# Attention on row and column tiles of TensorE in a decoder layer on one Trainium2 core

## The chip, the core and the metric

The kernel runs on one core of one Trainium2 chip. The metric is the device time of one execution in microseconds, lower is better. Engines are named as in the profile: PE is TensorE (PEld its weight loads), DVE is VectorE, ACT is ScalarE, POOL is GpSimd, SP is SyncE, which here only issues DMAs.

## What is computed

A decoder layer on eight sequences of 100 tokens with 256 features, in float32: a bidirectional state space mixer, cross attention to a context of 361 tokens per sequence, and a mixture of eight experts. The change touches the cross attention alone. Cut to it, with 16 heads of 16 features:

```python
v = (values @ Wv.T).reshape(N, -1, HEADS, HEAD_DIM)
k = (keys @ Wk.T).reshape(N, -1, HEADS, HEAD_DIM)
q = (query @ Wq.T).reshape(N, -1, HEADS, HEAD_DIM)
energy = jnp.einsum('nqhd,nkhd->nhqk', q, k)
attn = jax.nn.softmax(energy / HEAD_DIM ** 0.5, axis=-1)
out = jnp.einsum('nhqk,nkhd->nqhd', attn, v).reshape(N, Q, EMBED)
return out @ Wo.T + bo
```

## The kernel before

The program is written out engine by engine, with semaphores between them; nothing is scheduled by a tool, each engine runs its instructions in the order of the code. Four stages follow each other: projections and convolution of the mixer, its scan over 256 steps (the longest), attention, and the experts.

Attention goes sequence by sequence (`b`), and in a sequence by eight groups `g` of two heads (`attend`). Features lie on partitions: head h holds 16 of them, so a tile of 128 partitions holds eight heads, and there are two such tiles (`m`). Keys and values of the next sequence are made between the groups of the present one. Numbers with the precision of float32 are split into a high and a low part of a faster type (`three`: high by high, high by low, low by high), for queries, keys, context and their weights.

- **Queries.** ScalarE copies the high part, VectorE makes the low part (`high_queries`, `low_queries`). GpSimd spreads them (`spread_queries`, L666): for each head a block of 100 columns in which the 112 rows of the other heads are zero. So a matmul over all 128 rows gives the scores of one head.
- **Scores** (`scores`, L1011 by `three`): for each of two heads three matmuls with 100 weight columns and 362 streamed columns, into one PSUM bank per head.
- **Softmax.** VectorE takes the maxima of two heads (`maxima`, L1626) and scales and negates them (L1629, `shift`); ScalarE takes the exponential with that bias and accumulates the sum (`mass`, L901), one instruction a head and a read of the accumulator behind it.
- **Turning** (`turn_probs`, L1170): six transposes per group; VectorE copies one head's result out (L1637), ScalarE the other's (L910).
- **Weighing** (`weigh_values`, L1186): the turned probabilities are the weights (100 columns), the values of a head are streamed (16 columns); an fp32 matmul is two passes, so twelve passes a group. Heads come out token-major.
- **Normalising.** VectorE takes the reciprocal of 16 sums per token (L1641) and multiplies (L1644), TensorE turns the heads back (`turn_heads`, L1195), VectorE copies (L1651), TensorE projects them (`project_heads`, L1202, two fp32 matmuls), VectorE adds (L1659).

The order on TensorE is: turn group g, scores of group g+2, keys or values of the next sequence (groups 2 to 5), weigh group g. Turning g+2 must wait for the exponentials of g+2 and for both copies of g+1. Sequences 1 to 6 run in a hardware loop on TensorE, ScalarE, VectorE and GpSimd. Before attention GpSimd splits weights and contexts and adds the output bias to the residual (L674).

The profile's names: `ps` is PSUM, `x_tok` the residual, `q_blk_h/_l` the spread queries, `kT_h/_l` the keys. Forms read out<-in; in a matmul's form 128*100 is rows by weight columns, and behind it rows by streamed columns.

## Time and profile before

| | us |
|---|---|
| median of 3 runs | 1297.92 (1297.28 to 1300.14) |
| the profiled execution | 1293.94 |
| its span, from the first to the last instruction | 1292.2 |
| TensorE busy in it | 1033.0 (80%) |
| VectorE busy | 925.3 (72%) |
| GpSimd busy | 782.5 (61%) |
| ScalarE busy | 542.0 (42%) |

The span's four stages have different limits, so shares over the span say little about one of them. Attention lies at about 830 to 1058 us; what it costs is read from that stretch. Times in the views are from the span's start. A row of the timeline merges instructions of one kind that follow each other.

### The profile page before, as it was taken

Reading aid. Unit: us, or ns where it says so; the run is one execution under the profiler, and the core shown is the slowest. Engines: PE = TensorE matmul, PEld = TensorE weight load, DVE = VectorE, ACT = ScalarE, POOL = GpSimd, SP = SyncE. Lnnn points to the kernel's source line nnn. Section 1 sums busy time; section 2 is a strip of 40 time slices with the busy share of each in tenths; the row PEclk is TensorE's granted clock in tenths of the full one; section 3 lists DMA queues with packets and bytes.
Section 4 is the critical chain, followed back from the end, with each engine's and each line's share of the span. In section 5 each row is a group of like instructions: output and inputs, shape, how many; then the busy total and the mean of one; then the engine's idle time right before and its main releaser. Section 6 shows DMA issues by size and latency. Waiting matters only on the chain.

```text
span 1292.2 us, 14793 instructions
## 1 busy us (share of the span) xinstructions
PE 1033.0 (80%) x4832; PEld 705.2 (55%) x4832; DVE 925.3 (72%) x1068; ACT 542.0 (42%) x1188; POOL 782.5 (61%) x469
## 2 busy tenths in 40 slices
PE   7596676767667676676765779889999979899996
PEld 5243333433334333343332447779999966499995
DVE  6978998998989989999999993666666652021111
ACT  2686443443444434444444431244444433133231
POOL 4255998998998989989899890555223000402112
...
DMA packets 95706, 131.70 MB, mean 102 GB/s; under 512 B 12153, under 2 KB 89098, under 8 KB 95626
## 3 DMA queue, kind: packets, MB, share of 16 engines
...
## 4 chain that ended last, share of the span: by engine, by line
PE 37%; DVE 27%; issue 26%; POOL 5%; ACT 1%; SPq 1%; another core or an unknown queue 1%; DMA 1%; DVEq 0%; POOLq 0%; ACTq 0%
DVE states L1538 13%; DVE states L1550 10%; PE ps L1011 6%; PE ps L1378 6%; PE ps L1392 5%; PE ps L1186 4%; PE ps L1004 3%; PE ps L1170 2%; PE ps L1078 2%; PE ps L1069 2%; PE ps L1315 2%; PE ps L1324 2%; POOL dt L596 1%; POOL dtu L600 1%; POOL row_sel L565 1%
## 5 line engine op out<-in xcount | busy, mean ns | idle before, releaser
L619 POOL TENSOR_TENSOR states<-states,c_row 128x800 f32<-128x800 f32 x255 | 474.4, 1883 | 58.7 <-DVE states L1550 57.7
L1550 DVE TENSOR_TENSOR_SCAN states<-ps,states 128x800 f32<-128x800 f32 x256 | 462.7, 1830 | 0.0
L852 ACT ACTIVATE ps<-dt,neg_a 128x396 f32<-128x396 f32 x512 | 283.4, 585 | 361.8 <-DVE states L1550 361.8
L1078 PE MATMUL ps<-states,ident 128*128 128x400 f32 x1024 | 417.1, 543 | 1.9 <-POOL states L619 1.9
L1078 PEld LDWEIGHTS ps<-states,ident 128*128 128x128 f32 x1024 | 211.2, 210 | 142.0 <-issue 52.4
L1538 DVE TENSOR_TENSOR states<-dtu,ps 128x800 f32<-128x800 f32 x192 | 188.1, 980 | 31.1 <-PE ps L1060 28.3
L1060 PE MATMUL ps<-b_parts,row_sel 96*128 96x400 bf16 x192 | 69.0, 360 | 161.8 <-DVE states L1538 156.3
L1060 PEld LDWEIGHTS ps<-b_parts,row_sel 96*128 96x128 bf16 x192 | 18.9, 99 | 237.6 <-DVE states L1538 220.1
L610 POOL TENSOR_TENSOR states<-dtu,b_row 128x800 f32<-128x800 f32 x64 | 121.1, 1892 | 0.0
L901 ACT ACTIVATE probs<-ps,shift 100x361 f32<-100x361 f32 x128 | 70.8, 559 | 99.1 <-DVE shift L1629 99.1
...
L971 ACT ACTIVATE hid_tile<-ps,w_tile 128x128 f32<-128x128 f32 x160 | 45.6, 368 | 97.8 <-PE ps L1378 97.8
L1186 PEld LDWEIGHTS ps<-v,probsT 128*100 128x100 f32 (+1 forms) x768 | 75.4, 168 | 10.9 <-issue 8.3
L666 POOL TENSOR_TENSOR q_blk_h<-qT_h,head_mask 128x800 fp32r<-128x800 f32 x16 | 24.4, 1524 | 91.2 <-PE ps L1011 81.4
L1186 PE MATMUL ps<-v,probsT 128*100 128x16 f32 (+1 forms) x768 | 74.9, 236 | 5.4 <-ACT probsT L910 4.6
L1378 PEld LDWEIGHTS ps<-x_turned,w_tile 128*128 128x128 f32 x640 | 75.4, 194 | 2.2 <-issue 1.3
L1378 PE MATMUL ps<-x_turned,w_tile 128*128 128x128 f32 x640 | 75.7, 277 | 1.0 <-DVE out_tok L1789 1.0
L1626 DVE TENSOR_REDUCE neg_max<-ps 100x2 f32<-100x722 f32 x64 | 58.1, 908 | 25.5 <-PE ps L1011 25.5
...
L1392 PE MATMUL ps<-w_tile,hid_tile 128*128 128x256 f32 x320 | 72.2, 379 | 0.0
L1392 PEld LDWEIGHTS ps<-w_tile,hid_tile 128*128 128x128 f32 x320 | 59.3, 190 | 7.3
L994 PE MATMUL ps<-xT,win 128*128 128x400 f32 x128 | 52.8, 579 | 7.4 <-ACT u_pad L753 7.4
...
## 6 DMA issues: line engine op xcount, KB each, us to landing
c_row<-rows SPq DMA_DIRECT2D x256, 200.0 KB, 3.1
...
```

What stands on the lines that cost most here:

```text
L610: nc.gpsimd.tensor_tensor(states[i % RING][:].rearrange("p (c t) -> p c t", c=CP), dtu[d][:, cp * CP:(cp + 1) * CP, chunk(q)], b_row[turn ...
L619: nc.gpsimd.tensor_tensor(st, st, c_row[i % C_SLOTS][:].unsqueeze(1).broadcast_to([P, CP, TQ]), ALU.mult).then_inc(product_ready, 1)
L852: nc.scalar.activation(seqs(decay[i % DECAYS][:, j * TQ:(j + 1) * TQ])[:, :, 1:], seqs(dt_sb[d][:, c, chunk(q)])[:, :, 1:], ACT.Exp, scale ...
L901: nc.scalar.activation(probs[g % 2][:, j, 0:S], ps[0:L, g % 2 * 2 + j, 0:S], ACT.Exp, bias=shift[:, r, h:h + 1], scale=HD ** -0.5, accum_o ...
L1011: mm = nc.tensor.matmul(to, w[i], x[j], start=(first and n == 0), stop=(last and n == 2))
L1060: nc.tensor.matmul(ps[:, 6 + turn % 2, 0:TQ], row_sel[:, n, :], b_parts[d][:, chunk(q)], start=True, stop=True).then_inc(b_bank_ready, 1)
L1078: mm = nc.tensor.matmul(ps[:, j, 0:TQ], ident[:], states[i % RING][:, j * TQ:(j + 1) * TQ], start=False, stop=(i % N == N - 1), skip_group ...
L1186: mm = nc.tensor.matmul(ps[0:L, 6, h * HD:(h + 1) * HD], probsT[g % 2][j][0:size, kt * L:(kt + 1) * L], v_sb[r][0:size, kt, h * HD:(h + 1) ...
L1378: mm = nc.tensor.matmul(ps[:, hid_bank(k, ft), ft % 4 * P:(ft % 4 + 1) * P], w[:, W1_AT + m * F + ft * P:W1_AT + m * F + (ft + 1) * P], x_ ...
L1392: mm = nc.tensor.matmul(ps[:, 6 + k % 2, 0:D], hid_tile[k % 2][:, ft, :], w[:, W2_AT + ft * D:W2_AT + (ft + 1) * D], start=(ft == 0), stop ...
L1538: nc.vector.tensor_tensor(states[i % RING][:].rearrange("p (c t) -> p c t", c=CP), dtu[d][:, cp * CP:(cp + 1) * CP, chunk(q)], ps[:, bank_ ...
L1550: nc.vector.tensor_tensor_scan(st, decay[i % DECAYS], st, 0.0, ALU.mult, ALU.add).then_inc(scan_done, 1)
```

## The change

Queries are kept twice, once masked to the even heads of each 32 rows and once to the odd ones (`q_part`, masks `par_mask`, which also carry the factor 1/4 of the scores), so that a matmul over 32 rows gives the scores of one head. The two heads of a group lie in different 32-row tiles. GpSimd no longer spreads queries. Values are kept in 32 columns a head: 16 values, a one, and zeros; they become the weights, and the turned probabilities are streamed (100 columns), into a 32-partition strip of PSUM for each head. The column of ones makes the sums. The heads come out feature-major, so they are not turned; one matmul with a selecting matrix spreads the sums over each head's partitions, and the reciprocal and the product run on 128x400. The output weights are spread over four blocks to match, which makes the projection four fp32 matmuls. Maxima come negated, without the scaling. TensorE's loop over sequences is written out.

```diff
-KEY_BANK = 7
+KEY_BANK, HEAD_BANK = 7, 6
+QUAD = 32
+PAR = QUAD // HD
+BLOCKS = H // (P // QUAD)
+HEAD_CONSTS = 7
...
-        qT_part = [sb(f"qT_{n}", [P, KD, T], F32R, scope=attn) for n in "hl"]
-        q_blk = [[sb(f"q_blk_{n}{r}", [P, KD, HT, L], F32R, scope=attn) for n in "hl"] for r in range(2)]
+        q_part = [[sb(f"q_{n}{i}", [P, KD, T], F32R, scope=attn) for n in "hl"] for i in range(PAR)]
...
-        v_sb = [sb(f"v{r}", [P, KT, D], scope=attn) for r in range(2)]
+        v_sb = [sb(f"v{r}", [P, KT, H, QUAD], scope=attn) for r in range(2)]
...
-        neg_max, shift, mass, inv_mass = (
-            sb(n, [L, 2, H], scope=attn) for n in ("neg_max", "shift", "mass", "inv_mass"))
-        heads_tok = sb("heads_tok", [L, D], scope=attn)
-        headsT = sb("headsT", [P, KD, L], scope=attn)
+        neg_max = sb("neg_max", [L, 2, H], scope=attn)
+        heads_raw, inv_mass, headsT = (sb(n, [P, BLOCKS, L], scope=attn) for n in ("heads_raw", "inv_mass", "headsT"))
+        mass_sel = sb("mass_sel", [P, P], scope=attn)
...
+        def head_at(pos):
+
+            m, rest = divmod(pos, HT)
+            par, j = divmod(rest, P // QUAD)
+            return m, j, par
...
-            for w_dram, w_sbuf in ((wqT, wq_sb), (wkT, wk_sb), (wvT, wv_sb), (woT, wo_sb)):
+            for w_dram, w_sbuf in ((wqT, wq_sb), (wkT, wk_sb), (wvT, wv_sb)):
...
+            sp.wait_ge(wo_zeroed, 1)
+            for m in range(KD):
+                for j in range(P // QUAD):
+                    sp.dma_start(wo_sb[j * QUAD:j * QUAD + HD, m * PAR:(m + 1) * PAR, :],
+                                 woT.rearrange("(m j r i) e -> m j i r e", m=KD, j=P // QUAD, r=PAR)[m, j]
+                                 ).then_inc(wo_in, 16)
...
-            fill(head_mask[:], 1.0)
+            fill(head_mask[:], HD ** -0.5)
...
-            pool.wait_ge(attnw_in, 16 * 4)
+            job_result(pool, ("mix", DIRS - 1, B // 2 - 1))
+            nc.gpsimd.memset(wo_sb[:], 0.0).then_inc(wo_zeroed, 1)
+            nc.gpsimd.memset(mass_sel[:], 0.0).then_inc(sel_ready, 1)
+            for r in range(2):
+                nc.gpsimd.memset(v_sb[r][:], 0.0).then_inc(v_zeroed, 1)
+            pool.wait_ge(sel_ready, 1)
+            selected = mass_sel[:].rearrange("p (j i) -> p j i", i=QUAD)
+            nc.gpsimd.affine_select(out=selected, in_=selected, compare_op=ALU.not_equal, fill=1.0, base=-HD,
+                                    pattern=[[-QUAD, P // QUAD], [0, QUAD]], channel_multiplier=1
+                                    ).then_inc(sel_ready, 1)
+            pool.wait_ge(v_zeroed, 2)
+            for r in range(2):
+                nc.gpsimd.memset(v_sb[r][:, :, :, HD:HD + 1], 1.0).then_inc(v_zeroed, 1)
+            pool.wait_ge(attnw_in, 16 * 3)
...
-            def spread_queries(b, r):
-
-                for m in range(KD):
-                    if isinstance(b, int):
-                        job_copied(pool, ("qT", m, b // BQ))
-                    for part, block in zip(qT_part, q_blk[r]):
-                        nc.gpsimd.tensor_tensor(
-                            block[:, m],
-                            part[:, m, bass.ds(b * L, L)].bitcast(F32).unsqueeze(1).broadcast_to([P, HT, L]),
-                            head_mask[:].unsqueeze(2).broadcast_to([P, HT, L]), ALU.mult).then_inc(q_blk_ready, 1)
-
-            spread_queries(0, 0)
...
-            spread_queries(1, 1)
...
-            def prepare(b, r, next_loads=None):
-
-                pool.wait_ge(scores_ready, GROUPS * b - GROUPS)
-                spread_queries(b, r)
-                if next_loads is not None:
-                    split_context(b + 1, 1 - r, next_loads)
+            def prepare(b, r, next_loads):
+
+                split_context(b + 1, 1 - r, next_loads)
...
-                nc.scalar.activation(qT_part[0][:, m, chunk(q)], bank(("qT", m, q))[:, 0:TQ], ACT.Copy
-                                     ).then_inc(q_high, 1)
-
+                for i in range(PAR):
+                    ins = nc.scalar.activation(q_part[i][0][:, m, chunk(q)], bank(("qT", m, q))[:, 0:TQ],
+                                               ACT.Identity, scale=par_mask[:, i:i + 1])
+                ins.then_inc(q_high, 1)
...
-                act.wait_ge(shift_ready, GROUPS * b + (g + 1))
+                act.wait_ge(max_ready, GROUPS * b + (g + 1))
...
-                                         bias=shift[:, r, h:h + 1], scale=HD ** -0.5,
-                                         accum_out=mass[:, r, h:h + 1]).then_inc(probs_ready, 1)
+                                         bias=neg_max[:, r, h:h + 1]).then_inc(probs_ready, 1)
...
             def scores(b, r, g):
                 m = 2 * g // HT
-                pe.wait_ge(q_blk_ready, 2 * KD * b + 2 * (m + 1))
                 if g % (GROUPS // KD) == 0:
                     pe.wait_ge(k_copied, 2 * b + (m + 1))
                 if not isinstance(b, int) or GROUPS * b + g >= 2:
 
                     pe.wait_ge(probs_ready, 2 * GROUPS * b + (2 * g - 2))
-                for j in range(2):
-                    mm = three(ps[0:L, g % 2 * 2 + j, 0:SE], [part[:, m, (2 * g + j) % HT, :] for part in q_blk[r]],
-                               [part[:, m, :] for part in kT_part[r]], True, True)
+                for n, (hi, lo) in enumerate(((0, 0), (0, 1), (1, 0))):
+                    for i in range(2):
+                        _, j, par = head_at(2 * g + i)
+                        rows = slice(j * QUAD, (j + 1) * QUAD)
+                        mm = nc.tensor.matmul(ps[0:L, g % 2 * 2 + i, 0:SE],
+                                              q_part[par][hi][rows, m, b * L:(b + 1) * L],
+                                              kT_part[r][lo][rows, m, :], start=(n == 0), stop=(n == 2))
                 mm.then_inc(scores_ready, 1)
...
-                for j in range(2):
-                    h = 2 * g + j
-                    for kt in range(KT):
-                        size = P if kt < KT - 1 else SL
-                        mm = nc.tensor.matmul(ps[0:L, 6, h * HD:(h + 1) * HD],
-                                              probsT[g % 2][j][0:size, kt * L:(kt + 1) * L],
-                                              v_sb[r][0:size, kt, h * HD:(h + 1) * HD],
+                for kt in range(KT):
+                    size = P if kt < KT - 1 else SL
+                    for i in range(2):
+                        m, j, par = head_at(2 * g + i)
+                        block = (2 * g + i) // (P // QUAD)
+                        mm = nc.tensor.matmul(ps[j * QUAD:(j + 1) * QUAD, HEAD_BANK, block * L:(block + 1) * L],
+                                              v_sb[r][0:size, kt, m * HT + j * PAR + par, :],
+                                              probsT[g % 2][i][0:size, kt * L:(kt + 1) * L],
                                               start=(kt == 0), stop=(kt == KT - 1))
                 mm.then_inc(pv_done, 1)
...
-            def turn_heads(b):
+            def spread_mass(b):
                 pe.wait_ge(heads_ready, b + 1)
-                for m in range(KD):
-                    mm = nc.tensor.transpose(ps[:, KEY_BANK, m * L:(m + 1) * L], heads_tok[:, tile(m)],
-                                             ident[0:L, 0:L])
-                mm.then_inc(headsT_done, 1)
+                nc.tensor.matmul(ps[:, KEY_BANK, 0:BLOCKS * L], mass_sel[:], heads_raw[:].rearrange("p k t -> p (k t)"),
+                                 start=True, stop=True).then_inc(mass_spread, 1)
 
             def project_heads(b):
                 pe.wait_ge(headsT_copied, b + 1)
-                for m in range(KD):
-                    mm = nc.tensor.matmul(ps[0:L, KEY_BANK, 0:D], headsT[:, m, :], wo_sb[:, m, :], start=(m == 0),
-                                          stop=(m == KD - 1))
+                if b == 0:
+                    pe.wait_ge(wo_in, 16 * KD * (P // QUAD))
+                for k in range(BLOCKS):
+                    mm = nc.tensor.matmul(ps[0:L, KEY_BANK, 0:D], headsT[:, k, :], wo_sb[:, k, :], start=(k == 0),
+                                          stop=(k == BLOCKS - 1))
                 mm.then_inc(wo_done, 1)
...
-            with pe.Fori(0, B // 2 - 1) as i:
-                attend(2 * i + 1, 1)
-                attend(2 * i + 2, 0)
+            for b in range(1, B - 1):
+                attend(b, b % 2)
...
-            dve.wait_ge(consts, TURNS)
+            dve.wait_ge(consts, HEAD_CONSTS)
+            nc.vector.tensor_reduce(par_mask[:], head_mask[:].rearrange("p (j r) -> p r j", r=PAR), AX.X, ALU.add
+                                    ).then_inc(mask_ready, 1)
...
-                nc.vector.tensor_tensor(qT_part[1][:, m, chunk(q)], bank(("qT", m, q))[:, 0:TQ],
-                                        qT_part[0][:, m, chunk(q)].bitcast(F32), ALU.subtract
-                                        ).then_inc(copied["v"], 1)
-
+                for i in range(PAR):
+                    ins = nc.vector.scalar_tensor_tensor(
+                        q_part[i][1][:, m, chunk(q)], bank(("qT", m, q))[:, 0:TQ], par_mask[:, i:i + 1],
+                        q_part[i][0][:, m, chunk(q)].bitcast(F32), ALU.mult, ALU.subtract)
+                ins.then_inc(copied["v"], 1)
...
             def maxima(b, r, g):
                 dve.wait_ge(scores_ready, GROUPS * b + (g + 1))
                 nc.vector.tensor_reduce(neg_max[:, r, 2 * g:2 * g + 2], ps[0:L, g % 2 * 2:g % 2 * 2 + 2, 0:S],
-                                        AX.X, ALU.max).then_inc(max_ready, 1)
-                dve.wait_ge(max_ready, GROUPS * b + (g + 1))
-                nc.vector.tensor_scalar(shift[:, r, 2 * g:2 * g + 2], neg_max[:, r, 2 * g:2 * g + 2],
-                                        -HD ** -0.5, None, ALU.mult).then_inc(shift_ready, 1)
+                                        AX.X, ALU.max, negate=True).then_inc(max_ready, 1)
...
-            def normalise_heads(b, r):
-                dve.wait_ge(probs_ready, 2 * GROUPS * b + 2 * GROUPS)
-                nc.vector.reciprocal(inv_mass[:, r, :], mass[:, r, :]).then_inc(inv_mass_ready, 1)
+            def copy_heads(b):
+                dve.wait_ge(pv_done, GROUPS * b + GROUPS)
+                nc.vector.tensor_copy(heads_raw[:].rearrange("p k t -> p (k t)"), ps[:, HEAD_BANK, 0:BLOCKS * L]
+                                      ).then_inc(heads_ready, 1)
+
+            def normalise_heads(b):
+                dve.wait_ge(mass_spread, b + 1)
+                nc.vector.reciprocal(inv_mass[:].rearrange("p k t -> p (k t)"), ps[:, KEY_BANK, 0:BLOCKS * L]
+                                     ).then_inc(inv_mass_ready, 1)
                 dve.wait_ge(inv_mass_ready, b + 1)
-                dve.wait_ge(pv_done, GROUPS * b + GROUPS)
-                nc.vector.tensor_tensor(heads_tok[:].rearrange("l (h e) -> l h e", h=H),
-                                        ps[0:L, 6, 0:D].rearrange("l (h e) -> l h e", h=H),
-                                        inv_mass[:, r, :].unsqueeze(2).broadcast_to([L, H, HD]), ALU.mult
-                                        ).then_inc(heads_ready, 1)
-
-            def copy_heads(b):
-                dve.wait_ge(headsT_done, b + 1)
-                nc.vector.tensor_copy(headsT[:].rearrange("p m t -> p (m t)"), ps[:, KEY_BANK, 0:KD * L]
-                                      ).then_inc(headsT_copied, 1)
+                nc.vector.tensor_tensor(headsT[:], heads_raw[:], inv_mass[:], ALU.mult).then_inc(headsT_copied, 1)
```

In the order of instructions the change shows at three places. TensorE, one group with neither keys nor values, in the middle of a sequence (turning, scores, weighing), before:

```order
L1170 MATMUL ps<-ident,probs 128x100 x6
L1011 MATMUL ps<-kT_h,q_blk_h 100x362
L1011 MATMUL ps<-kT_l,q_blk_h 100x362
L1011 MATMUL ps<-kT_h,q_blk_l 100x362
L1011 MATMUL ps<-kT_h,q_blk_h 100x362
L1011 MATMUL ps<-kT_l,q_blk_h 100x362
L1011 MATMUL ps<-kT_h,q_blk_l 100x362
```

and after, with the weighing and the next group's turning:

```order
L1191 MATMUL ps<-ident,probs 128x100 x6
L1179 MATMUL ps<-kT_h,q_h 100x362 x2
L1179 MATMUL ps<-kT_l,q_h 100x362 x2
L1179 MATMUL ps<-kT_h,q_l 100x362 x2
L1208 MATMUL ps<-probsT,v 32x100 x6
L1191 MATMUL ps<-ident,probs 128x100 x6
```

The six score matmuls now alternate between the two heads, each pair in two row tiles, and weighing writes 32 rows by 100 columns where it wrote 100 by 16.

VectorE, from the last maxima of a sequence's groups to the addition of the attention's output, before:

```order
L1626 TENSOR_REDUCE neg_max<-ps 100x2
L1629 TENSOR_SCALAR shift<-neg_max 100x2
L1641 RECIPROCAL inv_mass<-mass 100x16
L1644 TENSOR_TENSOR heads_tok<-ps,inv_mass 100x256
L1637 COPY probsT<-ps 128x300
L1626 TENSOR_REDUCE neg_max<-ps 100x2
L1629 TENSOR_SCALAR shift<-neg_max 100x2
L1651 COPY headsT<-ps 128x200
L1637 COPY probsT<-ps 128x300
L1626 TENSOR_REDUCE neg_max<-ps 100x2
L1629 TENSOR_SCALAR shift<-neg_max 100x2
L1659 TENSOR_TENSOR x_tok<-x_tok,ps 100x256
```

and after:

```order
L1654 TENSOR_REDUCE neg_max<-ps 100x2
L1666 COPY heads_raw<-ps 128x400
L1662 COPY probsT<-ps 128x300
L1654 TENSOR_REDUCE neg_max<-ps 100x2
L1671 RECIPROCAL inv_mass<-ps 128x400
L1674 TENSOR_TENSOR headsT<-heads_raw,inv_mass 128x400
L1662 COPY probsT<-ps 128x300
L1654 TENSOR_REDUCE neg_max<-ps 100x2
L1681 TENSOR_TENSOR x_tok<-x_tok,ps 100x256
```

The reciprocal moved behind the maxima of group 2 of the next sequence, on 128x400, with the product right behind it and ahead of the next copy.

GpSimd, from its last product of the scan to the split of the key weights, after (before, the row of L657 followed the first one directly, as L637):

```order
L652 TENSOR_TENSOR states<-states,c_row 128x400
L670 MEMSET wo_sb 128x1024
L671 MEMSET mass_sel 128x128
L673 MEMSET v 128x1536 x2
L676 AFFINE_SELECT mass_sel<-mass_sel 128x128
L681 MEMSET v 128x48 x2
L657 TENSOR_TENSOR wk_h<-wk_sb,one 128x512
```

Seven instructions stand between the scan and the splits.

## Rows read from the trace of the kernel before

**Rows 1.** Busy time of each engine in a stretch of attention, clock, DMA

```profile
core 0: us, PE busy (x) PEld busy (x) DVE busy (x) ACT busy (x) POOL busy (x), PEclk, DMA share, GB/s
900.00:950.00 50.00, 49.36 (x436) 47.53 (x435) 31.16 (x62) 24.59 (x79) 14.88 (x11) 1.00 0.06 16
```

**Rows 2.** Timeline of TensorE: start us, us, engine, line, out<-in, count

```profile
902.75 0.71 PE L1170 MATMUL ps<-ident,probs 100*128 100x100 f32 x6
...
904.28 1.02 PE L1202 MATMUL ps<-wo_sb,headsT 128*100 128x256 f32 x4
905.15 1.15 PE L1186 MATMUL ps<-v,probsT 128*100 128x16 f32 x12
...
913.33 0.71 PE L1170 MATMUL ps<-ident,probs 100*128 100x100 f32 x6
913.82 0.39 PE L1011 MATMUL ps<-kT_h,q_blk_h 128*100 128x362 f32 x1
...
914.86 0.29 PE L1011 MATMUL ps<-wv_h,ctx_h 128*128 128x256 f32 x1
...
916.29 1.15 PE L1186 MATMUL ps<-v,probsT 128*100 128x16 f32 x12
...
929.23 0.71 PE L1170 MATMUL ps<-ident,probs 100*128 100x100 f32 x6
```

**Rows 3.** Timeline of all engines, groups 6 and 7; waits in brackets

```profile
920.54 0.71 PE L1170 MATMUL ps<-ident,probs 100*128 100x100 f32 x6
...
922.27 0.91 DVE L1626 TENSOR_REDUCE neg_max<-ps 100x2 f32<-100x722 f32 x1 [0.52 <-PE ps L1011]
...
923.22 0.48 DVE L1629 TENSOR_SCALAR shift<-neg_max 100x2 f32<-100x2 f32 x1
...
923.81 0.56 ACT L901 ACTIVATE probs<-ps,shift 100x361 f32<-100x361 f32 x1 [1.53 <-DVE shift L1629]
...
924.27 0.19 ACT L901 ACTIVATION_READ_ACCUMULATOR probs<-ps,shift 100x1 f32 x1
...
924.89 0.42 ACT L910 ACTIVATE probsT<-ps 128x300 f32<-128x300 f32 x1
...
925.46 1.20 PE L1186 MATMUL ps<-v,probsT 128*100 128x16 f32 x12 [0.29 <-ACT probsT L910]
...
926.51 0.71 PE L1170 MATMUL ps<-ident,probs 100*128 100x100 f32 x6
```

**Rows 4.** Groups of VectorE by shape: busy us, mean ns, idle before, releaser

```profile
L1641 DVE RECIPROCAL inv_mass<-mass 100x16 f32<-100x16 f32 x8 | 1.9, 243 | 0.0
...
L1445 DVE RECIPROCAL rstd<-std 100x4 f32<-100x4 f32 x10 | 1.8, 178 | 7.7 <-ACT std L749 7.7
L1795 DVE COPY shared_sum<-ps 128x400 f32<-128x400 f32 x2 | 1.1, 575 | 31.1 <-PE ps L1345 31.1
```

**Rows 5.** Timeline of TensorE in the expert stage

```profile
1108.15 1.51 PE L1315 MATMUL ps<-xn3T,w_shared 128*128 128x400 f32 x4
1109.59 1.54 PE L1302 MATMUL ps<-ident,rows_src 100*9 100x100 f32 x16
1111.06 1.61 PE L1324 MATMUL ps<-hidden,w_shared 128*128 128x400 f32 x4
...
1128.61 2.95 PE L1345 MATMUL ps<-cwT,b_sb 9*128 9x400 f32 x8
1131.50 0.66 PE L1366 MATMUL ps<-ident,x_tile 128*128 128x128 f32 x4
```

**Rows 6.** As rows 1, while TensorE runs matmuls on 16 rows (form 16*128)

```profile
66.00:70.00 4.00, 4.00 (x7) 1.99 (x7) 3.00 (x7) 2.85 (x6) 0.00 (x0) 0.50 0.22 51
```

**Rows 7.** Timeline beside GpSimd's fill early on, and before attention's first turning

```profile
19.65 8.42 DVE L1470 TENSOR_SCALAR diag_d<-ident,vec 128x128 f32<-128x128 f32 x8
...
20.44 3.52 POOL L558 MEMSET row_sel<- 96x4096 bf16 x1 [16.16 <-DMA bias_tok<-in_bo]
...
839.95 3.66 DVE L1629 TENSOR_SCALAR shift<-neg_max 100x2 f32<-100x2 f32 x1
...
846.58 0.62 PE L1170 MATMUL ps<-ident,probs 100*128 100x100 f32 x5 [3.18 <-DVE qT_l L1604]
```

34 lines of the change are left out of this document (22 added, 12 removed).

## Prediction

> **What bounds the kernel now.** I read the stretches first, then TensorE's timeline in one sequence, then the waits behind its idle time. From 846 us to 1055 us the kernel does attention, one of the eight sequences after the other, and there TensorE is busy 49.4 of 50 us at full clock, VectorE 31.2, ScalarE 24.6, GpSimd 14.9 [rows 1]. So this stage belongs to TensorE, and its cost is read from where the same instruction comes back: transposing the probabilities of head pair 1 starts at 902.75 and, one sequence later, at 929.23, so a sequence takes 26.48 us [rows 2]. Inside a group (one pair of heads) the parts are: six transposes 0.49 us (913.33 to 913.82), six score matmuls 1.04 (to 914.86: 0.165 each and 0.06 for weights that weren't loaded ahead), the values of the next sequence 1.43 for twelve (so 0.71 for six), weighing the values, and elsewhere the output projection, 0.87 for four passes (904.28 to 905.15) [rows 2]. Keys are six matmuls of the scores' form, so 0.99.
>
> Not every group is full. Groups 6, 7 and 0 have little between scores and weighing, and there a loop of latencies decides: transposes of group g (920.54), scores of g+2, their maxima (922.27, 0.91 us), the shift (923.22), two exponentials (923.81), ScalarE's copy of the probabilities of g+1 (924.89, 0.42), weighing g+1 (925.46), transposes of g+2 (926.51): 5.97 us for two groups [rows 3]. In it the shift lasted 0.48 us where a free one takes 0.17, since GpSimd was spreading queries; without that the pair is 5.66.
>
> **Scores.** The block-masked queries on 128 rows become masked queries on 32 rows: the same six matmuls of 362 columns, three for each of two heads, but the two heads lie in different row tiles. If two tiles run at once, three slots of 0.165 replace six: 0.50 for 0.99. If not, nothing is gained. No row of before has two matmuls at different tile positions, so this is bounded from both sides, by 0.50 and 0.99; I take 0.50. The Trainium skill, "TensorE: Matmul & The Clock Gate", Part 3 (Measured speedup vs the span model), gives 3.07 times for four row tiles and 2.38 times for three column tiles; no run here shows it yet.
>
> **Weighing.** Twelve passes (an fp32 matmul is two) now load 100 weight columns to stream 16 columns: 1.05 us (925.46 to 926.51) [rows 3]. Afterwards each loads 32 and streams 100. The rows have exactly such passes, 9 weight columns and 100 streamed, at 0.086 us (1.54 us is 15 steps and one pass of 0.25) [rows 5]. Serial, twelve are 1.03, no gain. In two column tiles the second pass of one head runs beside the first of the other: seven slots, 0.60. I take 0.60, bound 1.03.
>
> **Switching.** This is the price that the change adds. Every group now goes from the whole array to row tiles to column tiles and back, with keys and values as one more change. Before has a handful of such changes [rows 5]: four matmuls from 1108.15 would end at 1109.49 at their pace of 0.336, the narrow ones start at 1109.59 (0.10); sixteen of them need 1.38 and the next line starts 1.47 later (0.09), and its first four last 1.61 instead of 1.51 (0.10 for weights that can't be loaded ahead). Eight matmuls on 9 rows need 2.69 and take 2.89: 0.20 in and out. So a change is 0.10, and behind it the first weights: 0.03 for 32 columns or the transposes, 0.10 for the whole array, and before the scores two loads of 100 columns, between 0.08 (the two at once) and 0.17 (twelve loads in 1.05, so 0.087 each, one after the other); I take 0.15 in the sum below and come back to it.
>
> **One sequence afterwards.** A plain group on TensorE: 0.49 + (0.10 + 0.15 + 0.50) + (0.10 + 0.03 + 0.60) + 0.13 = 2.10. Two groups with keys: 2 x (2.10 + 0.99 + 0.20) = 6.58. Two with values: 2.10 + 1.43 + 0.20 = 3.73 and 2.10 + 0.71 + 0.20 = 3.01. Groups 6 and 7 go by the loop: 0.49 + 0.10 + 0.15 + 0.50 + 0.17 for the last score to finish + 0.03, maxima 0.91 + 0.03, exponentials, copy 0.42, 0.15 until weighing, 0.60 + 0.13. The exponentials take 1.08 as a pair now (923.81 to 924.89) and lose two reads of the accumulator of 0.20 each [rows 3], most of which overlaps the exponential: 0.98, bounds 0.69 and 1.08. Sum 4.65. That is 1.3 less than 5.97, and TensorE waits 0.2 per group.
>
> Groups 0 and 1 of the next sequence carry the heads' end. Spreading the masses is one matmul of 400 columns, two passes, 0.67 + 0.20: group 0 is 2.97. Then VectorE, behind the maxima, takes a reciprocal of 128x400 where it took one of 100x16. A reciprocal of 4 columns is 178 ns and one of 16 is 243 [rows 4]: 5.4 ns for each further column, so 178 + 396 x 5.4 = 2.3 us. Its lower bound is the copy of 128x400, 0.57 [rows 4]; I take the slope. The multiply is another 0.57. From the transposes of group 0 on: maxima end 1.44 + 0.91 = 2.35, reciprocal 4.7, multiply 5.3, and only then the projection, now eight passes instead of four, 1.74 + 0.10 (TensorE alone would be there at 4.1), then 0.86 for weighing and the way back: 8.0 for groups 0 and 1. Total 6.58 + 3.73 + 3.01 + 4.65 + 8.0 = 25.97, against 26.48: **0.5 us less per sequence**, with half of TensorE's score and weighing work gone. With the reciprocal at 0.57 it would be 24.97.
> The Trainium skill, "VectorE: DVE Perf Modes" (First, the fixed hardware budget), says that the divide runs with a repeat count of 8; at the 0.96 GHz that it gives, 400 columns would be an estimated 3.3 us. Rows 4 say 5.4 ns, and the sum goes by them.
>
> **Around the sequences.** Seven periods: -3.7. The last sequence has groups 2 to 7 without keys or values, two and a half pairs at 5.66 - 4.65: -2.5. Groups 0 and 1 of the first one: one pair, -1.3. Before them TensorE stood 3.2 us at 846.58, because a shift lay 3.66 us behind GpSimd's bias addition [rows 7]; now there is no shift, and GpSimd, freed of 32 multiplies of 1.5 us, adds the bias some 6 us sooner. The queries now cost two ScalarE and two VectorE instructions for one, 1.1 us of it on this path: -2.0. The end: after the last weighing VectorE had 0.42 and 0.37 us of work and two transposes; now a copy of 0.57, the mass at half clock 1.5, reciprocal 2.3, multiply 0.57, less 0.5 for a shorter last weighing: +3.5. The longer projection hides behind the first half's normalisation.
> Two costs come from GpSimd blocking VectorE's SBUF-to-SBUF instructions. Eight scalings that need 1.6 us lasted 8.42 us beside a fill of 3.52 [rows 7]. At 806 us GpSimd now clears four tiles, some 4,200 columns at 0.86 ns (3.52 us for 4,096), 3.7 us while VectorE normalises what TensorE waits for; it would wait for about one of the two large fills, 1.3: +1.1, bounds 0 and 3.7. And the new sum of the mask stands ahead of those eight scalings, so one instruction fewer slips through before the fill: +0.5, bounds -1 and +1. The eight small loads of the output weights come on SP's queue behind the context and ahead of the shared weights, which wait for 828 us anyway, and nothing needs them for 30 us: 0. TensorE's loop written out takes away three branches at the ends of passes and register steps that TensorE's queue ran ahead of: 0.
> Sum: -3.7 - 2.5 - 1.3 - 2.0 + 3.5 + 1.1 + 0.5 = -4.4. If weights of two row tiles load together, the six full groups of each sequence save 0.07, about -3 in all; I take half, -1.5. That makes **-6**: the profiled execution (1293.9 with its ends) would be 1288, and against the median of 1297.9 the forecast is **1292**. By itself this case reaches from 1283 (quick reciprocal) to 1301 (the bounds of the clearing and of the weights).
>
> **The rivals.**
> The tiles don't overlap. Then only the switches are bought. Each group costs 0.49 + 0.43 more than above; groups 6 and 7 are then TensorE's (6.04 instead of 4.65) and 0 and 1 rise by 0.9: 26.0 + 3.7 + 1.4 + 0.9 = 32.0, or 5.5 more than before, seven times 38, and the ends add 4: 1340. The whole span between 0.5 us of gain and 5.5 of loss per sequence hangs on the share of slots that overlap, so this mechanism decides already where less than nine tenths of them do: at half, the kernel is some 18 us slower. Nothing in the profile speaks for or against it. That is the case on the other side.
> One of the two overlaps: 28.9 per sequence, 18 us more: 1316. Two-pass fp32 matmuls are the likelier ones to fail, since passes of one tile must follow each other.
> The clock falls. Sixteen matmuls on 16 rows ran at 0.50, with TensorE busy 4.00 of 4.00 us [rows 6], while this stage shows 1.00 [rows 1]. Afterwards half of the score and weighing time uses half of the array. At half clock the 19 us of matmul work per sequence double, 155 us for all; in a fifth of the stage it is 30 us: 1322 or more. Against it: transposes, keys and values stay whole, and the stage held 1.00 through weighing passes that streamed 16 columns.
> No change worth measuring: the forecast's mechanism, but the reciprocal and the clearing at their upper ends, 1297.
>
> **How the numbers follow.** Both overlap at full clock 0.66, with 1292; one 0.13, with 1316; none 0.12, with 1340; clock 0.09. A measurement of this kernel tells about 0.2% (2.6 us) from no change. Of the 0.66, 0.44 lie below 1295.3, 0.14 within 2.6 us of before, 0.08 above. So faster 0.44, same 0.14, slower 0.42. The range goes from 1283 to 1340; outside are most of the clock's case and the tails of the first.
>
> **What would show it.** Score matmuls of a pair starting within some 20 ns of each other at 0.165 per pair, weighing in about 0.6 us per group, and 0.1 us gaps at each change of shape confirm the first steps; equal spacing of 0.165 refutes. The reciprocal's row should read about 2,300 ns, and TensorE's longest idle time should stand before the projection and be put down to VectorE. Granted clock below 1.00 between 846 and 1050 us would make the forecast wrong, and so would changes of shape that cost twice as much: they stand 30 times in a sequence (three in a group, one more where keys, values, masses or the projection stand between), and 0.05 us each is 1.5 us, more than the whole gain.

## The result, and the profile after

| | us |
|---|---|
| median of 12 runs before | 1298.78 (1293.19 to 1300.78) |
| median of 12 runs after | 1289.78 (1287.41 to 1297.08) |
| ratio | 0.9946, 95% interval 0.9926 to 0.9966 |
| profiled execution after, and its span | 1289.13, 1287.4 |

The change makes the kernel 0.5% faster (0.7% by the medians). The twelve runs after spread over 10 us, and TensorE's clock goes with it: the four runs at 1295 to 1297 us have a mean granted clock of 0.906 to 0.909, the other eight, at 1287 to 1290.5, of 0.910 to 0.914. The kernel before spreads too, over 7.6 us. The profiled execution of before, 1293.94 us, is 4.8 below its median, that of after 0.7 below; so the two profiles differ by 4.8 us where the medians differ by 9.0, and what follows explains the 4.8.

**Two tiles work at once.** TensorE in groups 6 and 7 of a sequence, after. Columns as in [rows 2]; the bracket is what the engine waited for.

```profile
864.23 0.73 PE L1191 MATMUL ps<-ident,probs 100*128 100x100 f32 x6
864.89 0.41 PE L1179 MATMUL ps<-kT_h,q_h 32*100 32x362 f32 x2
865.14 0.33 PE L1179 MATMUL ps<-kT_l,q_h 32*100 32x362 f32 x2
865.30 0.33 PE L1179 MATMUL ps<-kT_h,q_l 32*100 32x362 f32 x2
865.56 0.71 PE L1208 MATMUL ps<-probsT,v 128*32 128x100 f32 x12
866.20 0.73 PE L1191 MATMUL ps<-ident,probs 100*128 100x100 f32 x6
```

A row with x2 is two score matmuls, one in each tile, that start together, and the next pair starts 0.16 us later (865.14, 865.30): two matmuls in a slot of 0.165, where in [rows 2] each took a slot of its own. From start to start, turning takes 0.66 us, the scores 0.67 and weighing 0.64, each with the change behind it: 1.97 us for a group that took 2.5. The first two weights of the scores load together too (PEld is the weight load):

```profile
864.89 0.16 PEld L1179 LDWEIGHTS ps<-kT_h,q_h 32*100 32x100 f32 x2
```

**The wait before the projection.** Groups 0 and 1, all engines, after:

```profile
896.62 2.66 DVE L1671 RECIPROCAL inv_mass<-ps 128x400 f32<-128x400 f32 x1
...
899.31 0.58 DVE L1674 TENSOR_TENSOR headsT<-heads_raw,inv_mass 128x400 f32<-128x400 f32 x1
...
899.94 2.98 PE L1224 MATMUL ps<-wo_sb,headsT 128*100 128x256 f32 x8 [1.38 <-DVE headsT L1674]
```

The waits of TensorE in attention (what waited, for what: us in total, times, longest) show that this one repeats, once behind each of the first seven sequences:

```profile
PE ps L1224 <- DVE headsT L1674: 9.7, 7, 1.4
PE ps L1208 <- ACT probsT L927: 5.2, 10, 0.6
```

**The clock behind it.** Busy time by stretch, columns as in [rows 1], clock third from the end:

```profile
896.00:900.00 4.00, 2.62 (x27) 1.51 (x25) 3.96 (x4) 1.44 (x3) 0.00 (x0) 1.00 0.00 0
900.00:904.00 4.00, 4.00 (x20) 2.46 (x20) 1.51 (x3) 1.01 (x2) 0.00 (x0) 0.59 0.00 0
904.00:908.00 4.00, 4.00 (x40) 3.11 (x40) 1.52 (x3) 1.80 (x4) 0.00 (x0) 0.98 0.00 0
```

Projection and the next weighing then run at half clock. Behind three of the seven waits it is so, behind four it isn't. One of each kind, by the starts of groups 1 and 2 (6.84 us and 5.32):

```profile
897.16 0.73 PE L1191 MATMUL ps<-ident,probs 100*128 100x100 f32 x6
904.00 0.53 PE L1191 MATMUL ps<-ident,probs 100*128 100x100 f32 x3
...
951.35 0.73 PE L1191 MATMUL ps<-ident,probs 100*128 100x100 f32 x6
956.67 0.73 PE L1191 MATMUL ps<-ident,probs 100*128 100x100 f32 x6
```

From start to start of each group's turning, in a sequence at full clock (us):

| group | 0 | 1 | 2 | 3 | 4 | 5 | 6 | 7 | sum |
|---|---|---|---|---|---|---|---|---|---|
| before | 2.72 | 3.40 | 3.52 | 3.64 | 3.97 | 3.25 | 2.93 | 3.04 | 26.5 |
| after | 2.84 | 5.33 | 3.16 | 3.17 | 3.59 | 2.86 | 1.98 | 2.60 | 25.5 |

**GpSimd's clearings.** After, VectorE and GpSimd (start, us):

```profile
806.68 2.70 POOL L673 MEMSET v<- 128x1536 f32 x2
...
808.17 1.23 DVE L1463 TENSOR_SCALAR var_eps<-moments 100x4 f32<-100x4 f32 x1
```

and the stretch behind it, before and after:

```profile
812.00:818.00 6.00, 6.00 (x26) 4.83 (x26) 1.21 (x3) 0.44 (x1) 5.55 (x9) 0.78 0.14 50
```

```profile
812.00:818.00 6.00, 6.00 (x22) 4.87 (x21) 1.77 (x3) 0.69 (x1) 5.76 (x10) 0.50 0.24 51
```

An instruction of 0.17 us (`var_eps`) lasted 1.23, until the second clearing was over; the gap on TensorE grew by as much (2.58 us for 1.52), and behind it the clock was at 0.50 where it had been at 0.78. From the end of this gap to the first queries' product TensorE needs 20.6 us, before 18.9.

**The tail.** Last weighing, and what follows, after:

```profile
1047.06 0.71 PE L1208 MATMUL ps<-probsT,v 128*32 128x100 f32 x12 [0.60 <-DVE probsT L1662]
1047.81 0.57 DVE L1666 COPY heads_raw<-ps 128x400 f32<-128x400 f32 x1 [0.84 <-PE ps L1208]
...
1048.44 0.94 PE L1216 MATMUL ps<-heads_raw,mass_sel 128*128 128x400 f32 x2 [0.67 <-DVE heads_raw L1666]
1049.41 2.66 DVE L1671 RECIPROCAL inv_mass<-ps 128x400 f32<-128x400 f32 x1 [1.03 <-PE ps L1216]
...
1052.74 3.74 PE L1224 MATMUL ps<-wo_sb,headsT 128*100 128x256 f32 x8 [3.36 <-DVE headsT L1674]
...
1056.58 0.42 DVE L1681 TENSOR_TENSOR x_tok<-x_tok,ps 100x256 f32<-100x256 f32 x1
```

### The profile page after: what moved, and what is told of

It reads as the page before. It is cut to its first block, busy times and chain, and to the rows that moved or that the text cites. A ratio compares the mean times of both kernels' runs of the same rounds, so it can differ in the third digit from the quotient of the medians.

```text
span 1287.4 us, 14434 instructions
## 1 busy us (share of the span) xinstructions
PE 1012.4 (79%) x4864; PEld 645.4 (50%) x4864; DVE 929.8 (72%) x1009; ACT 536.0 (42%) x1064; POOL 739.4 (57%) x444
## 4 chain that ended last, share of the span: by engine, by line
DVE 29%; issue 27%; PE 24%; DMA 10%; POOL 6%; ACT 1%; SPq 1%; DVEq 0%; POOLq 0%; ACTq 0%
DVE states L1561 13%; DVE states L1573 10%; DMA sums<-y_tile,x_tile 9%; PE ps L1021 3%; PE ps L1028 3%; PE ps L1208 3%; PE ps L1191 3%; PE ps L1095 2%; PE ps L1179 2%; PE ps L1086 2%; DVE inv_mass L1671 2%; POOL dt L616 1%; PE ps L1224 1%; POOL dtu L620 1%; POOL rows_by_slot L746 1%
## 5 line engine op out<-in xcount | busy, mean ns | idle before, releaser
L1561 DVE TENSOR_TENSOR states<-dtu,ps 128x800 f32<-128x800 f32 x192 | 185.4, 966 | 31.1 <-PE ps L1077 28.3
L919 ACT ACTIVATE probs<-ps,neg_max 100x361 f32<-100x361 f32 x128 | 64.9, 560 | 79.4 <-DVE neg_max L1654 79.4
L657 POOL TENSOR_TENSOR ctx_h<-ctx,one 128x722 fp32r<-128x722 f32 x8 | 11.1, 1390 | 107.4 <-PE ps L1028 94.9
L1825 DVE COPY x_turned<-ps 128x256 f32<-128x256 f32 x20 | 8.5, 425 | 67.7 <-PE ps L1387 67.7
L1837 DVE TENSOR_SCALAR y_tile<-ps,weight 128x256 f32<-128x256 f32 x20 | 9.7, 484 | 59.8 <-PE ps L1413 59.8
```

The lines of the kernel that those rows point to most:

```text
L919: nc.scalar.activation(probs[g % 2][:, j, 0:S], ps[0:L, g % 2 * 2 + j, 0:S], ACT.Exp, bias=neg_max[:, r, h:h + 1]).then_inc(probs_ready, 1)
L1561: nc.vector.tensor_tensor(states[i % RING][:].rearrange("p (c t) -> p c t", c=CP), dtu[d][:, cp * CP:(cp + 1) * CP, chunk(q)], ps[:, bank_ ...
```

## The experiments

Each median stands beside runs of the kernel before on the same chip, whose medians were 1297.3 to 1298.6 us. Ratios are to those.

### Is it overlap? One tile for both heads, and head by head

```diff
-            par, j = divmod(rest, P // QUAD)
+            j, par = divmod(rest, PAR)
...
-                        block = (2 * g + i) // (P // QUAD)
+                        block = m * PAR + par
```

> The two heads of a group lie in the same 32 rows and the same 32 columns (the pairing of heads is changed; weighing goes head by head), so nothing can overlap, while every matmul keeps its size and every change of shape stays. Theory (what the new forms gain is that two tiles work at once): three more score slots of 0.165 us and five more weighing slots of 0.086 us in a group, +0.92 us in each of groups 2 to 5, 1.2 in groups 6 and 7 together, 0.9 in groups 0 and 1, so +5.8 us per sequence and a median near 1335 us at full clock. Rival (a matmul on 32 rows or in 32 columns is quicker by itself): 1290 us. Second rival (with a quarter of the array at work at a time the clock falls, as in the run with the scores alone): half clock through attention, over 1400 us.

1340.85 us (1335.03 to 1342.17), ratio 1.0324 (1.0301 to 1.0347). Its TensorE, a plain group:

```profile
944.61 0.73 PE L1191 MATMUL ps<-ident,probs 100*128 100x100 f32 x6
945.27 0.57 PE L1179 MATMUL ps<-kT_h,q_h 32*100 32x362 f32 x2
945.68 0.48 PE L1179 MATMUL ps<-kT_l,q_h 32*100 32x362 f32 x2
946.01 0.48 PE L1179 MATMUL ps<-kT_h,q_l 32*100 32x362 f32 x2
946.43 1.22 PE L1208 MATMUL ps<-probsT,v 128*32 128x100 f32 x12
```

A pair of scores now takes 0.33 us from start to next start where it took 0.165, and weighing 1.15 to the next turning instead of 0.64. Sizes are the same, so the whole gain of the new forms is overlap: a sequence takes 31.9 us instead of 25.5, and the medians differ by 51. This is the rival "no overlap" of the prediction: its 32.0 us per sequence is right. That its total of 1340 is met to the microsecond is luck, since this execution has some 8 us at half clock in the first sequence (granted clock 0.74 from 847 to 880 us), which that sum had not.

```diff
-                for n, (hi, lo) in enumerate(((0, 0), (0, 1), (1, 0))):
-                    for i in range(2):
+                for i in range(2):
+                    for n, (hi, lo) in enumerate(((0, 0), (0, 1), (1, 0))):
```

and `i` ahead of `kt` in `weigh_values` in the same way.

> The kernel after, with the matmuls of a group in another order: all three score matmuls of the first head, then those of the second, and weighing likewise. Tiles, sizes and changes of shape are those of after. Theory (only neighbours in the queue overlap): scores take five slots of 0.165 us instead of three (+0.33), weighing eleven of 0.086 instead of seven (+0.34); +0.67 in each of groups 2 to 5, +0.7 in groups 6 and 7 together, +0.7 in groups 0 and 1, so +4 us per sequence and a median near 1321 us. Rival (each tile has its own queue and the second head catches up): 1290 us. Second rival (the gain is not overlap): 1290 us as well, told apart by the starts of the matmuls.

1299.74 us (1293.82 to 1302.84), ratio 1.0004 (0.9986 to 1.0021). The theory fails for the scores and in size for weighing, and the rivals' 1290 fails too. Scores lose nothing, weighing loses 0.20:

```profile
932.47 0.41 PE L1179 MATMUL ps<-kT_h,q_h 32*100 32x362 f32 x2
932.72 0.33 PE L1179 MATMUL ps<-kT_l,q_h 32*100 32x362 f32 x2
932.89 0.32 PE L1179 MATMUL ps<-kT_h,q_l 32*100 32x362 f32 x2
...
934.33 0.91 PE L1208 MATMUL ps<-probsT,v 128*32 128x100 f32 x12
```

The timeline lists matmuls by their start, and the second head's first still starts with the first head's first, though two more of the first head stand between them in the program. So a pair needn't be neighbours: the other tile's work is reached past three matmuls at once, and past the six passes of a head's weighing 0.20 us late. One sequence takes 26.7 us instead of 25.5, 1.2 more, where I had expected 4.

### Which half pays? Scores alone, values alone

```diff
-                for kt in range(KT):
-                    size = P if kt < KT - 1 else SL
-                    for i in range(2):
-                        m, j, par = head_at(2 * g + i)
...
-                        mm = nc.tensor.matmul(ps[j * QUAD:(j + 1) * QUAD, HEAD_BANK, block * L:(block + 1) * L],
+                for i in range(2):
+                    m, j, par = head_at(2 * g + i)
+                    h = m * HT + j * PAR + par
...
+                        mm = nc.tensor.matmul(ps[0:L, HEAD_BANK, h * HD:(h + 1) * HD],
+                                              probsT[g % 2][i][0:size, kt * L:(kt + 1) * L],
+                                              v_sb[r][0:size, kt, h * HD:(h + 1) * HD],
```

and the heads' end, the sums and the loads of before with it.

> Masked queries on 32 rows, negated maxima and the unrolled loop as in the kernel after; weighing, sums, heads and projection as in the kernel before (100 weight columns, 16 streamed; reciprocal on 100x16; no clearings on GpSimd). Theory (the scores pay, and the half for the values gives its gain back in the reciprocal, the longer projection, the clearings and the clock): groups 2 to 5 about 0.25 us shorter than before each, groups 6 and 7 0.75 together, groups 0 and 1 0.4, so 2 us less per sequence than before and a median near 1281 us, below the kernel after. Rival (both halves pay, the switches eat the one as the other): between before and after, 1294 us; TensorE busy without a gap and at full clock in either case.

1422.71 us (1421.08 to 1424.52), ratio 1.0972 (1.0940 to 1.1004): 125 us slower than before, and neither theory had it. The stretch 910 to 940 us of this kernel, and of the next one:

```profile
910.00:940.00 30.00, 30.00 (x157) 25.21 (x158) 10.33 (x18) 8.81 (x27) 2.97 (x2) 0.50 0.05 13
```

```profile
910.00:940.00 30.00, 29.67 (x274) 25.71 (x273) 17.36 (x29) 15.80 (x49) 2.98 (x2) 1.00 0.05 13
```

TensorE is busy 30 of 30 us and at half clock, and stays so from the second sequence to the last, 44.4 us each. The next kernel streams 64 columns of the values in a pass instead of 16, and nothing else differs; its heads come out wrong:

```diff
-                        mm = nc.tensor.matmul(ps[0:L, HEAD_BANK, h * HD:(h + 1) * HD],
+                        mm = nc.tensor.matmul(ps[0:L, HEAD_BANK, at:at + 64],
...
-                                              v_sb[r][0:size, kt, h * HD:(h + 1) * HD],
+                                              v_sb[r][0:size, kt, at:at + 64],
```

> The kernel with the scores alone in small tiles (label scores_only), and each weighing pass streams 64 columns of the values instead of 16, so that results of other heads are overwritten: the heads are wrong, the instructions, their order and their waits are the same. At full clock a pass is bound by its 100 weight columns (0.087 us) either way. Theory (it was the weighing's 16 streamed columns, next to scores on 32 rows, that left TensorE too little at work to keep its clock, not the small tiles): full clock in most of attention and a median between 1275 and 1290 us. Rival (the small tiles bring the clock down, whatever streams beside them, unless the weights too are in small tiles): half clock throughout, the passes bound by their weights, and 1423 us as before.

1286.37 us (1279.54 to 1294.54), ratio 0.9916 (0.9888 to 0.9944), as the theory had it. More work per instruction, 136 us less time. The weighing of both, by shape (busy us, mean ns):

```profile
L1186 PE MATMUL ps<-v,probsT 128*100 128x16 f32 x128 | 25.4, 319 | 0.0
```

```profile
L1187 PE MATMUL ps<-v,probsT 128*100 128x64 f32 x264 | 33.6, 250 | 1.3 <-ACT probsT L906 1.3
```

So small tiles do not lower the clock by themselves (one_tile kept 1.00 with a quarter of the array at work), and passes that stream 16 columns do not either while the scores fill the array [rows 1]. Both together do. In the first sequence this kernel too runs at half clock, from 846 to 865 us; why isn't tested. At full clock the scores alone take 24.7 us a sequence.

The other half, in `scores` and with `spread_queries` back on GpSimd:

```diff
-                                              q_part[par][hi][rows, m, b * L:(b + 1) * L],
-                                              kT_part[r][lo][rows, m, :], start=(n == 0), stop=(n == 2))
+                    mm = three(ps[0:L, g % 2 * 2 + i, 0:SE], [part[:, m, j * PAR + par, :] for part in q_blk[r]],
+                               [part[:, m, :] for part in kT_part[r]], True, True)
```

> The other half alone: values as weights in 32 columns, sums by the column of ones, spreading, reciprocal and projection as in the kernel after; scores on 128 rows with queries spread by GpSimd as in the kernel before. Theory A (the clock fell in the run with the scores alone because its weighing streamed 16 columns between scores on 32 rows; here scores fill the array): full clock but for stretches behind the projection's wait; groups 2 to 5 0.35 us shorter than before each, groups 6 and 7 0.7 together, groups 0 and 1 2.4 longer: +0.3 us per sequence, a median near 1301 us. Theory B (any small tile brings the clock down if it stands beside other work of little activity): half clock through attention, 1400 us or more.

1294.42 us (1292.46 to 1298.89), ratio 0.9974 (0.9962 to 0.9986), full clock through attention; 26.65 us a sequence, groups 0 and 1 8.45 of it. Theory A holds on the clock, and was 7 us too high on the time: the first sequence is 3.8 us shorter than before's, and the expert stage gives 2 us, which the sum had not. The halves don't add up: alone they give +125 and -4 us, together -9. Wide weighing is what keeps the clock for the small scores.

### Does the wait for the reciprocal bring the clock down?

```diff
-                nc.vector.reciprocal(inv_mass[:].rearrange("p k t -> p (k t)"), ps[:, KEY_BANK, 0:BLOCKS * L]
+                nc.vector.tensor_copy(inv_mass[:].rearrange("p k t -> p (k t)"), ps[:, KEY_BANK, 0:BLOCKS * L]
```

> The kernel after with a plain copy of 128x400 where the reciprocal stood, so the heads are not divided by their sums; nothing else differs. Theory (the reciprocal of 2.66 us makes TensorE wait 1.38 us before each projection, and that wait brings the clock down behind it in some sequences): the wait disappears, 7 x 1.38 = 9.7 us, the tail is 2.1 us shorter, no stretch at half clock behind a projection, 4.5 us more: a median near 1273 us and no run above 1277. Rival (the clock has nothing to do with the wait): the half-clock stretches stay, 1278 us. Second rival (another wait stands right behind, the copies of pair 1): 1285 us or more.

1276.82 us (1276.36 to 1278.04), ratio 0.9850 (0.9823 to 0.9877), and its four runs lie within 1.7 us. This kernel leaves the division by the sums out. TensorE's waits for `headsT` shrink to one, at the tail:

```profile
PE ps L1224 <- DVE headsT L1674: 1.3, 1, 1.3
```

The stretches at half clock behind the projections are gone and the runs no longer spread. It is 3.8 above the theory; the profiled execution has another stretch at half clock, in the first sequence, which is 3.9 us longer than in after.

```diff
+                    for _ in range(7):
+                        nc.tensor.matmul(ps[:, HEAD_BANK, 400:500], mass_sel[:], heads_raw[:, 0, :], start=True,
+                                         stop=True)
                     project_heads(b)
```

> The kernel after with seven more matmuls of 128 weight columns and 100 streamed columns (float32, 0.17 us each) between the scores of group 3 and the projection of the previous heads, in each sequence but the last; their result goes to unused columns of PSUM. TensorE is then busy in 1.2 of the 1.39 us that it waited; no step is taken out. Theory (the idle 1.4 us bring the clock down, at some places, in some executions): granted clock 1.00 behind every projection but for the first sequence, the spread between runs shrinks from 10 us to about 3, median near 1285 to 1287 us. Rival (the clock falls for the small tiles, or for something outside): half-clock stretches stay, median 1290 us with runs at 1296 us as before.

1289.28 us (1281.07 to 1290.27), ratio 0.9924 (0.9902 to 0.9946). No stretch at half clock behind a projection in the profiled execution, and no run above 1290.3; but the spread is 9 us where theory had 3, and the median didn't fall. Each sequence costs 0.1 us more, and the first sequence's stretch (3.9 us) is in this execution and was not in the profiled one of after. That filling the wait protects the clock is not shown by this: a kernel further down, `clear_late`, keeps the same seven waits unfilled,

```profile
PE ps L1223 <- DVE headsT L1673: 9.7, 7, 1.4
```

and has no stretch at half clock behind any of them either; headwise has one behind its seven waits of 1.2 us. So a wait of this length is followed by half clock only sometimes. What taking it away does is shown: the five kernels without it (copy_for_recip, warm, reordered, reordered_late, warm_late, of four or five runs each) have no stretch behind a projection, and runs within 1.4 to 3.5 us.

```diff
             queries(1)
+            pe.wait_ge(probs_ready, 4)
+            for _ in range(13):
+                nc.tensor.matmul(ps[:, 0, 400:500], mass_sel[:], ident[:, 0:L], start=True, stop=True)
```

> The kernel with the projection one group later (label reordered), and thirteen more matmuls of 128 weight columns and 100 streamed columns behind the last queries, where TensorE waits 2.6 us before the first turning; their result goes to unused columns of PSUM. Theory (that idle time brings the half-clock stretch of groups 1 and 2 of the first sequence: they took 3.49 and 5.47 us where later ones take 1.98 and 5.25): groups 0 to 2 of the first sequence about 1.5 to 3 us shorter, median near 1277 us. Rival (the stretch comes from the turn of the work to small tiles itself): no change, 1279 us.

This is the kernel `reordered`, shown below, with thirteen more matmuls. 1275.88 us (1275.26 to 1278.12) against 1279.24 (1278.39 to 1279.81) without them: 3.4 us less by medians from two chips; by the ratios to before on each, 0.9839 (0.9825 to 0.9854) and 0.9849 (0.9834 to 0.9863), it is little more than 1 us and within their intervals. The profiled executions differ by 4.2. The same 4 us of the first sequence, without and with:

```profile
848.00:852.00 4.00, 4.00 (x34) 2.80 (x29) 1.96 (x3) 1.70 (x4) 0.00 (x0) 0.51 1.09 326
```

```profile
848.00:852.00 4.00, 3.52 (x44) 2.46 (x38) 2.35 (x4) 2.65 (x6) 0.00 (x0) 1.00 1.10 330
```

Groups 0 to 2 of the first sequence take 7.5 us instead of 11.0. Such a stretch is in six of the nine profiled executions that leave this wait unfilled (scores_only and wide_stream aside), and in neither of the two that fill it. So thirteen matmuls with no use most likely shorten the kernel, as theory had it; by how much isn't settled.

### Do the clearings cost what they seem to?

```diff
-            nc.gpsimd.memset(wo_sb[:], 0.0).then_inc(wo_zeroed, 1)
...
             for n, (part, raw) in enumerate(((wk_part, wk_sb), (wv_part, wv_sb))):
                 split_into([t[:] for t in part], raw[:], kv_split, 2 * n)
...
-            for b in range(2):
-                split_context(b, b, 1)
+            nc.gpsimd.memset(wo_sb[:], 0.0).then_inc(wo_zeroed, 1)
...
+            split_context(0, 0, 1)
```

> The kernel after with the seven clearing and selecting instructions of GpSimd behind the splits of the key and value weights instead of ahead of them, and the split of the second context behind the addition of the output bias. Theory (a clearing holds VectorE's SBUF instruction for 1.06 us at 808.2 us, and the longer gap on TensorE brings its clock down for 1.6 us more): the first turning of attention 2.6 us earlier, median near 1287 us. Rival 1 (only the 1.06 us come back, the clock falls anyway): 1288.7. Rival 2 (the clearings now stand in the way of the contexts or of the next normalisation): 1290 or more.

1292.14 us (1283.68 to 1295.08), ratio 0.9947 (0.9929 to 0.9965). The median is that of the second rival and 5 us above the theory, but with a spread of 11 us it says little. In the profiled execution `var_eps` is back at 0.17 us:

```profile
807.60 0.17 DVE L1462 TENSOR_SCALAR var_eps<-moments 100x4 f32<-100x4 f32 x1
```

and the first queries' product starts at 828.6 us instead of 831.9; 0.6 of this it had already ahead of the clearings, so the edit gives 2.7, as the theory had it: 1.06 of the wait and 1.6 of the clock behind it. Against it stands the first sequence's stretch at half clock, 3.9 us, which this execution has and that of after has not.

All profiled executions together say how firm the second part is. From the end of TensorE's gap to the first queries' product it needs 20.0 to 20.6 us in seven of the eight executions whose gap is 2.58 us or more, and 18.9 in one (`filled_bank6`); where the gap is 1.52 us, it needs 18.9 in five of six, before among them, and 20.5 in one (`reordered_late`). So the longer gap mostly brings the lower clock with it, not always.

### A better order

The projection moves behind the scores of group 4, and the reciprocal is cut in two with `copy_probs` of group 1 between the halves:

```diff
                     scores(*nxt, 3)
-                    project_heads(b)
                     weigh_values(*nxt, 1)
+                    turn_probs(b + 1, 2)
+                    scores(*nxt, 4)
+                    project_heads(b)
+                    weigh_values(*nxt, 2)
+                    if b + 2 < B:
+                        keys(b + 2, r, 0)
```

> The kernel after with the projection of the heads one group later: it stands behind the scores of group 4, with the weighing of group 2 behind it and then the keys; the reciprocal is two instructions of 128x200 with the copy of the probabilities of group 1 between them. Nothing is left out. Theory (TensorE has enough other work for the 2.66 us of the reciprocal): the 1.38 us wait disappears in seven sequences, 9.7 us, and with it the half-clock stretches, 4.5 us; a median near 1275 us, groups 0 to 2 together 10 us instead of 11.3. Rival (a new wait takes its place: the exponentials of group 3, whose maxima come 2.4 us later, or the keys behind VectorE's addition): 1283 us or more, with TensorE idle before the turning of group 3 or before the keys.

1279.24 us (1278.39 to 1279.81), ratio 0.9849 (0.9834 to 0.9863). TensorE no longer waits for the heads between sequences (the 3.4 us at the tail stay), and at six places 0.2 us for the low part of the keys; groups 0 to 2 take 10.1 us for the 11.3 of after. VectorE's halves, with the copy that TensorE's weighing needs between them:

```profile
898.66 1.41 DVE L1686 RECIPROCAL inv_mass<-ps 128x200 f32<-128x200 f32 x1
...
899.99 0.46 DVE L1671 COPY probsT<-ps 128x300 f32<-128x300 f32 x1
...
900.36 1.40 DVE L1686 RECIPROCAL inv_mass<-ps 128x200 f32<-128x200 f32 x1
```

It is 4 us above the expectation, which is the first sequence's stretch at half clock: the kernel `warm` is this one with that mended.

> Both edits of this call together: projection one group later and GpSimd's clearings behind the splits of the weights. If the two gains are independent, as the theory has it, 14 + 2.6 us below the kernel after: a median near 1273 us. Rival (the clearing's cost was an accident of the clock in one execution): the same as with the reordering alone, within 1 us.

1278.09 us (1277.43 to 1280.45), ratio 0.9844 (0.9830 to 0.9859): 1.1 less, close to the rival, and with ranges that overlap not clear of noise. The profiled execution has the wait of 1.06 us back, but the lower clock behind the shorter gap all the same.

> The projection one group later, the thirteen matmuls in the wait before the first turning, and GpSimd's clearings behind the splits of the weights. The first two gave 1275.9 us; the third, alone on top of the reordering, took 1.1 us. Theory (the gains are independent): a median near 1274.8 us and all runs within 3 us. Rival (an earlier start meets another half-clock stretch): 1276 us or more.

1273.64 us (1271.88 to 1275.37), ratio 0.9813 (0.9794 to 0.9832): the fastest kernel here, 1.9% below before and 16 us below after. It is 2.2 us below `warm` by medians from two chips, with profiled spans that are equal (1273.6 and 1273.5 us), so what the clearings are worth in the whole time stays open. Attention stands at full clock from 846 us, in its first group, to 1034 us, in its last:

```profile
846.00:1034.00 188.00, 178.43 (x1794) 131.76 (x1792) 125.96 (x189) 92.40 (x202) 18.95 (x13) 1.00 0.10 28
```

## Why the prediction was right, and where only its sum was

The median, 1289.8, lies 2.2 us below the forecast. Some luck is in that. The medians differ by 9.0 us where 6 were forecast, and the two profiled executions, on which the sum can be checked, by 4.8: the forecast lies between the two. The terms, from one profiled execution to the other (rounded; "attention" ends at the start of the last weighing, as in the prediction's sum):

| term | forecast | measured |
|---|---|---|
| mask's sum ahead of the early scalings | +0.5 | -0.1 |
| clearings, VectorE's wait | +1.1 | +1.1 |
| clock behind it | not in the sum | +1.7 |
| from the first queries to the first turning | -2.0 | -2.2 |
| attention up to the last weighing | -9.0 | -6.3 |
| from there to the shared expert | +3.5 | +2.5 |
| expert stage | 0 | -1.4 |
| sum | -6 | -4.8 |

- **Scores and weighing overlap**: right, and shown by one_tile. Three slots for the scores, as the prediction had it, and by the sum six for weighing where it had seven: 0.52 and 0.12 for the change, which is what one_tile has beside its twelve slots of 0.086, make the 0.64. The Trainium skill, "TensorE: Matmul & The Clock Gate", Part 3 (Measured speedup vs the span model), gives 3.07 times for four row tiles; two tiles give 2.0 here (0.165 us a pair for 0.33), and the trace agrees in kind.
- **Switching**: slightly too dear. From the turning's start to the scores it is 0.66 us for a forecast 0.74 (0.49 + 0.10 + 0.15): the two weights ahead of the scores load together in 0.16, and the lower bound of 0.08 gives 0.67. From the scores to weighing it is 0.67 for 0.63. A plain group takes 1.98 us, not 2.10; the latency loop 4.58, not 4.65; groups 2 to 5 12.8, not 13.3.
- **The reciprocal**: 2.66 us, not 2.3. The slope from two rows of few columns was the part of the term that was too small: 128x200 takes 1.41 and 128x400 2.66, so 6.3 ns a column, not 5.4. Those two rows also read SBUF and these read PSUM; which of the two makes the difference isn't tested. Groups 0 and 1 take 8.17 for the 8.0 of the sum, and TensorE's wait stands where the prediction put it. The divide of the Trainium skill's "VectorE: DVE Perf Modes" (First, the fixed hardware budget) gave an estimated 3.3; the row lies between.
- **Per sequence** this is 25.5 for the forecast 25.97: 1.0 us of gain for 0.5.
- **The clock**: the step that failed. The sum took full clock for granted, and the prediction named a clock below 1.00 in attention as a sign that would make it wrong; that sign came, 0.97 from 846 to 1055 us (before 1.00), and the forecast held in spite of it. The rival gave the cause to half of the array standing idle, at 30 us or more with a chance of 0.09. What happened is smaller and stands elsewhere: a wait of 1.4 us and, behind three of seven, half clock, 1.6 us each, 4.7 in all. It took back what the overlap gave beyond the forecast: without it attention would stand at -11.0 for the -9.0. So two errors of opposite sign meet in a good sum. The rival in its own form is real too, but not for this kernel: scores_only is it, at +125 us.
- **Clearings**: right in place and size, and incomplete. Behind the longer gap on TensorE the clock was lower (0.50 for 0.78, 1.7 us), as in seven of the eight executions with such a gap.
- **Tail**: 1.0 us too dear. The last weighing is 0.9 us shorter, not 0.5 (before's lasted 1.61 us, longer than the 1.20 of the others; after's takes 0.71), and the masses take 0.94, not 1.5; against that stands the reciprocal. The longer projection, 3.74 us at half clock, ends with the normalisation at 1056.5 us and hides behind it.
- **Expert stage**: 1.4 us that nothing forecast. TensorE enters it at a higher clock. What takes TensorE the stage's first 12.4 us in before takes 9.4 here, and 1.6 of that gain is lost again later, at a place that wasn't looked for. All this is seen and not tested. The stretch before, and after:

```profile
1062.00:1070.00 8.00, 5.75 (x15) 3.78 (x16) 1.85 (x8) 3.35 (x7) 0.00 (x0) 0.50 0.01 2
```

```profile
1062.00:1070.00 8.00, 8.00 (x47) 5.82 (x46) 0.45 (x2) 3.19 (x5) 0.00 (x0) 0.84 0.00 0
```
